# One gather fetched by SyncE row by row, subtractions in four pieces, and a tile's back transposes moved in a DLRM tower on one Trainium2 core

## What is computed

```
e = stack([tbl_f[ids[:, f]] for f in range(26)], axis=1)        # 512 x 26 x 128
combined = concatenate([e, dense[:, None, :]], axis=1)          # 512 x 27 x 128
z = einsum('bfd,bgd->bfg', combined, combined)[:, i < j]        # 351 pair products
h = concatenate([z, dense], axis=1)                             # 512 x 479
h = relu(h @ W_top1 + b_top1); h = relu(h @ W_top2 + b_top2)    # 512, then 256 wide
y = h @ W_top3                                                  # 512 x 1
```

## Time and profile before

| | us |
|---|---|
| median of 3 runs | 108.18 (108.18 to 108.19) |
| the profiled execution, device time | 108.26 |
| its span, first to last instruction | 106.4 |
| TensorE busy (granted clock full throughout) | 99.0 |
| DVE busy | 79.4 |
| ACT busy | 73.9 |
| POOL busy | 67.7 |
| 64 gathers on POOL: busy, and idle between them | 66.8 and 19.2 |

### The profile page before, as it was taken

One profiled execution on the slowest core, in us unless ns is written; L12 is line 12 of the kernel. 1 busy time (PEld: TensorE's weight loads), 2 busy tenths in 40 slices (PEclk: granted clock), 3 DMA queues, 4 the chain that ended last, 5 costly groups with the idle time before them and its releaser, 6 DMA issues.

```text
span 106.4 us, 2498 instructions
## 1 busy us (share of the span) xinstructions
PE 99.0 (93%) x998; PEld 78.6 (74%) x998; DVE 79.4 (75%) x141; ACT 73.9 (69%) x147; POOL 67.7 (64%) x72
## 2 busy tenths in 40 slices
PE   5999999999999999999989979889999985999991
PEld 1246765765686676789789967879999974899991
DVE  6899999999999999999758994951058712586120
ACT  4499999999999999999167772632257631374430
POOL 3777777777877778777777777777777773000000
PEclk9999999999999999999999999999999999999999
DMA  4861826655374654899122222111222211000000
GB/s 54 317 237 49 230 74 214 158 188 180 122 223 76 226 163 131 252 398 265 51 55 54 66 59 54 51 49 49 55 60 65 54 49 49 6 0 0 6 0 1
DMA packets 5239, 11.68 MB, mean 110 GB/s; under 512 B 1998, under 2 KB 2520, under 8 KB 5228
## 3 DMA queue, kind: packets, MB, share of 16 engines
q1 hardware_dynamic: 3160, 7.31, 21.6%
q0 software_dynamic: 2048, 4.20, 14.4%
q10 hardware_dynamic: 20, 0.02, 0.1%
HBM read 11.48 MB, written 0.00 MB: 108 GB/s over the span
## 4 chain that ended last, share of the span: by engine, by line
POOL 61%; issue 18%; PE 12%; DMA 4%; POOLq 1%; DVE 0%; ACT 0%
POOL rows L313 61%; PE gram_ps L670 3%; DMA rows<-table,ids_sb 2%; DMA ids_sb<-ids 2%; PE top_ps L737 2%; PE tr_ps L712 1%; POOLq L112 1%; PE act_ps L749 1%; PE dve_ps L749 1%; PE top_ps L762 1%; PE dve_ps L726 1%; PE dve_ps L712 1%; PE act_ps L712 1%; PE gram_ps L706 0%; PE tr_ps L683 0%
## 5 line engine op out<-in xcount | busy, mean ns | idle before, releaser
L313 POOL DMA_INDIRECT rows<-table,ids_sb x64 | 66.8, 1044 | 20.7 <-issue 19.2
L630 PE MATMUL gram_ps<-onehot,high 128*128 128x512 f32 x82 | 22.2, 405 | 0.1
L638 PE MATMUL gram_ps<-onehot,low 128*128 128x512 f32 x82 | 21.6, 406 | 0.0
L630 PEld LDWEIGHTS gram_ps<-onehot,high 128*128 128x128 f32 x82 | 14.5, 188 | 6.1 <-DVE onehot L483 2.8
L638 PEld LDWEIGHTS gram_ps<-onehot,low 128*128 128x128 f32 x82 | 14.5, 188 | 4.7 <-issue 1.8
L670 PE MATMUL gram_ps<-xt 128*58 128x52 f32 x512 | 15.1, 217 | 1.1 <-issue 1.1
L670 PEld LDWEIGHTS gram_ps<-xt 128*58 128x58 f32 x512 | 14.3, 133 | 2.0 <-issue 1.5
L483 DVE TENSOR_TENSOR onehot<-dve_ps,row_f 128x1536 fp32r<-128x1536 f32 (+1 forms) x10 | 15.2, 1524 | 0.0
L522 DVE COPY gram_sb<-gram_ps 26x208 f32<-26x208 f32 x32 | 12.0, 376 | 3.9 <-PE gram_ps L670 1.8
L483 DVE TENSOR_TENSOR onehot<-gram_ps,row_f 128x1024 fp32r<-128x1024 f32 (+1 forms) x10 | 14.8, 1478 | 0.0
L341 ACT ACTIVATE gram_sb<-gram_ps 26x208 f32<-26x208 f32 x32 | 10.7, 334 | 5.1 <-PE gram_ps L670 3.7
(11 more groups left out here) (99 smaller groups left out, 111.1 us busy)
## 6 DMA issues: line engine op xcount, KB each, us to landing
table<-table SPq DMA_DIRECT2D x9, 512.0 KB, 3.7
rows<-table,ids_sb POOLq DMA_INDIRECT x64, 2.9
w1p_sb<-w_pairs SPq DMA_DIRECT2D x1, 768.0 KB
table<-table SPq DMA_DIRECT2D x1, 640.0 KB
w_sb<-w SPq DMA_DIRECT2D x1, 512.0 KB
dense_sb<-dense SPq DMA_DIRECT2D x1, 256.0 KB, 5.8
w1d_sb<-w_dense SPq DMA_DIRECT2D x1, 256.0 KB
ids_sb<-ids SPq DMA_DIRECT2D x1, 52.0 KB, 2.0
```

What stands on the lines that cost most here:

```text
L313: pool.indirect_dma_start(rows[:, t, s - 1, :], None, tables[f], bass.IndirectOffsetOnAxis(ids_sb[:, t, f:f + 1], 0)).then_inc(gathered[t] ...
L630: pe.matmul(pick_ps[b][:], high[:, b, c, :], onehot[:, b, c, :], start=(c == 0), stop=False)
L638: last = pe.matmul(pick_ps[b][:], low[:, b, c, :], onehot[:, b, c, :], start=False, stop=(c == CHUNKS[o] - 1))
```

## The change

POOL no longer gathers slot 16 of tile 3. Its 128 rows are fetched by SP instead: the host lays the 128 ids out in a line, `ids_in_line`, which is loaded into `row_ids`; for each row SP loads one id into a register and issues a DMA of one row of 512 B at that address. Ten rows are issued ahead of the load of the third table, seven behind the load of each table from the third on, and the other 62 behind the weights. `gathered[3][4]` is waited for at 16 x 128.

The subtraction is made in 4 pieces, DVE's second one-hot instruction is split in two, and the pieces stand between the one-hot instructions. DVE's share of the shared chunk falls from 272 to 192 columns for the tables of 8 chunks. The transposes back of tile 0 go into `top_ps`, stand between the third and fourth set of `gram(1)` on TensorE, and are copied out by ACT alone. The clearing of `xt` moves: tile 2 to ACT ahead of the tables, tile 3 to DVE ahead of `gram(0)`. Three waits are finer.

```diff
-DVE_CHUNKS = {8: ((0, 1), (2, 3, 4)), 10: ((0, 1, 2), (3, 4, 5))}
-SHARED_COLS = {8: 272, 10: 368}
-DVE_PARTS = 3
+DVE_CHUNKS = {8: ((0, 1), (2,), (3, 4)), 10: ((0, 1, 2), (3,), (4, 5))}
+SHARED_COLS = {8: 192, 10: 368}
+DVE_PARTS = 4
-REST = 2
+REST = 4
+LAST_SLOT = NG
+ROWS_A_TABLE = 7
+ROWS_FIRST = 10
...
         def _(sp):
             sp.dma_start(ids_sb[:], ids.rearrange("(p t) f -> p t f", t=TILES)).then_inc(ids_in, 16)
+            def rows_by_address(at):
+                f = SLOT_FIELD[LAST_SLOT]
+                for p in at:
+                    r = sp.value_load(row_ids[0:1, p:p + 1], min_val=0, max_val=tables[f].shape[0] - 1)
+                    sp.dma_start(rows[p:p + 1, TILES - 1, LAST_SLOT - 1, :], tables[f][bass.ds(r, 1)]
+                                 ).then_inc(gathered[TILES - 1][-1], 16)
...
+                if o == TABLES:
+                    sp.wait_ge(row_ids_in, 16)
+                    rows_by_address(range(0, ROWS_FIRST))
                 if o >= TABLES:
                     sp.wait_ge(low_ready, REST * (o - TABLES + 1))
                 sp.dma_start(table[:, o % TABLES, 0:CHUNKS[o]], tables[f].rearrange("(p c) d -> p c d", c=CHUNKS[o])
                              ).then_inc(table_in[o % TABLES], 16)
                 if o == TABLES - 1:
                     sp.dma_start(dense_sb[:], dense.rearrange("(p t) d -> p t d", t=TILES)).then_inc(dense_in, 16)
+                    sp.dma_start(row_ids[:], ids_in_line).then_inc(row_ids_in, 16)
+                if o >= TABLES:
+                    rows_by_address(range(ROWS_FIRST + (o - TABLES) * ROWS_A_TABLE, ROWS_FIRST + (o - TABLES + 1) * ROWS_A_TABLE))
                 if o == WEIGHTS_AFTER:
...
+            rows_by_address(range(ROWS_FIRST + (NO - TABLES) * ROWS_A_TABLE, P))
...
                     for s in BANK_SLOTS[t][n]:
+                        if (t, s) == (TILES - 1, LAST_SLOT):
+                            continue
...
+            def back_first():
+                act.wait_ge(back_ready, 1)
+                act.activation(pairs_t[:], top_ps[:, 0:NC, :], ACT.Copy).then_inc(back_out_act, 1)
...
             def first_layer(n):
-                act.wait_ge(h1_ready, n * (N1 // P))
+                act.wait_ge(h1_ready, n * (N1 // P) - (1 if n == TILES - 1 else 2))
...
+            act.wait_ge(zeros_ready, 1)
+            act.activation(xt[:, 2, :, N_SLOTS:PAD], zeros[:, 0:1].rearrange("d (p s) -> d p s", p=1
+                                                                           ).to_broadcast([P, P, PAD - N_SLOTS]), ACT.Copy
+                           ).then_inc(pad_zero, 1)
...
-            gram(1)
-            back(1)
+            gram(1, range(SETS - 1))
+            back_first()
+            gram(1, (SETS - 1,))
...
             for o in range(NO - 1):
                 dve.wait_ge(high_ready, o + 1)
                 rest(o, 0)
...
                 whole_chunks(o + 1, 0)
                 rest(o, 1)
                 shared_chunk(o + 1)
+                rest(o, 2)
                 whole_chunks(o + 1, 1)
+                rest(o, 3)
+                whole_chunks(o + 1, 2)
...
+            dve.memset(xt[:, 3, :, N_SLOTS:PAD], 0.0).then_inc(pad_zero, 1)
             transposed(0, (3,))
...
-            dve.memset(xt[:, 2, :, N_SLOTS:PAD], 0.0).then_inc(pad_zero, 1)
             gram(1)
-            back(1)
             transposed(2, (0,))
-            dve.memset(xt[:, 3, :, N_SLOTS:PAD], 0.0).then_inc(pad_zero, 1)
...
                         pe.wait_ge(onehot_dve, DVE_PARTS * o + 3)
+                    elif c == DVE_CHUNKS[CHUNKS[o]][2][0]:
+                        pe.wait_ge(onehot_dve, DVE_PARTS * o + 4)
...
-                    pe.wait_ge(gathered[t][n], 16 * len(slots))
+                    pe.wait_ge(gathered[t][n], 16 * (P if slots[-1] == LAST_SLOT and t == TILES - 1 else len(slots)))
...
             def dense_part(t, parts=range(N1 // P)):
-                if t:
-                    pe.wait_ge(h1_out_act, 2 * t)
-                    pe.wait_ge(h1_out_dve, 2 * t)
                 ps = h1_banks(t)
                 for m in parts:
+                    if t:
+                        pe.wait_ge((h1_out_act, h1_out_dve)[m // 2], 2 * t)
...
+            def back_first():
+                pe.wait_ge(packed_act, 1)
+                pe.wait_ge(packed_dve, 1)
+                for c in range(NC):
+                    last = pe.transpose(top_ps[:, c, :], packed[:, c * P:(c + 1) * P], ident[:])
+                last.then_inc(back_ready, 1)
...
-            pe.wait_ge(pad_zero, 2)
+            pe.wait_ge(pad_zero, TILES)
...
-            gram(1)
+            gram(1, range(SETS - 1))
+            back_first()
+            gram(1, (SETS - 1,))
             transposes(2, (0, 1))
-            back(0)
             first_layer(0, range(N1 // P))
...
+        "ids_in_line": np.ascontiguousarray(a["ids"][TILES - 1::TILES, SLOT_FIELD[LAST_SLOT]].reshape(1, P)),
```

More of the change, by code:

```diff
@@ L108, with tower @@
 I32 = mybir.dt.int32
-def tower(nc, dense, ids, ids_by_field, tables, w1_pairs, w1_dense, b1, w2, b2, w3, out):
+def tower(nc, dense, ids, ids_by_field, ids_in_line, tables, w1_pairs, w1_dense, b1, w2, b2, w3, out):
     with ExitStack() as ctx:
@@ L146, in tower @@
         field_ids = sb("field_ids", [NO, B], I32)
+        row_ids = sb("row_ids", [1, P], I32)
         field_ids16 = sb("field_ids16", [P, B], F16)
@@ L183, in tower @@
         ids_in = sem("ids_in")
+        row_ids_in = sem("row_ids_in")
         dense_in = sem("dense_in")
@@ L503, in _ @@
             whole_chunks(0, 1)
+            whole_chunks(0, 2)
             for o in range(NO - 1):
@@ L651, in transposes, with gram @@
                     last.then_inc(tr_ready, 1)
-            def gram(t):
+            def gram(t, sets=range(SETS)):
                 pe.wait_ge(tr_out_dve, TR_OUT[0][t + 1])
                 pe.wait_ge(tr_out_act, TR_OUT[1][t + 1])
-                for s in range(SETS):
+                for s in sets:
                     n = t * SETS + s
@@ L686, in back @@
             def back(t):
-                pe.wait_ge(gram_out_act, max(t + 1, 2) * SETS)
-                pe.wait_ge(gram_out_dve, max(t + 1, 2) * SETS)
+                pe.wait_ge(gram_out_act, (t + 1) * SETS)
+                pe.wait_ge(gram_out_dve, (t + 1) * SETS)
                 pe.wait_ge(packed_act, t + 1)
@@ L722, in first_layer @@
                 pe.wait_ge(back_out_act, t + 1)
-                pe.wait_ge(back_out_dve, t + 1)
+                if t:
+                    pe.wait_ge(back_out_dve, t)
                 for m in parts:
@@ L813, in _ @@
             first_layer(1, range(N1 // P))
-            pe.wait_ge(pad_zero, TILES)
             gram(2)
@@ L881 @@
     out = nc.dram_tensor("y", (B, 1), F32, kind="ExternalOutput").ap()
-    tower(nc, ap["dense"], ap["ids"], ap["ids_by_field"], [ap[f"table{f}"] for f in range(N_FIELDS)],
+    tower(nc, ap["dense"], ap["ids"], ap["ids_by_field"], ap["ids_in_line"], [ap[f"table{f}"] for f in range(N_FIELDS)],
           ap["w1_pairs"], ap["w1_dense"], ap["b1"], ap["w2"], ap["b2"], ap["w3"], out)
```

## The result

| us | before | after |
|---|---|---|
| median of 4 runs | 108.19 (108.18 to 108.19) | 196.85 (196.78 to 197.52) |
| span of the profiled execution | 106.4 | 194.9 |
| TensorE busy | 99.0 | 111.7 |
| POOL's gathers, busy | 66.8 (64) | 61.7 (63) |
| last POOL gather started | 88.02 (slot 16; slot 15 at 86.77) | 82.39 (slot 15) |

The time is 1.821 times that of before (95% interval 1.817 to 1.825).

A forecast was written before the change was run, and what follows sets the result against it. POOL's gather pace, locked to DVE's subtractions, was taken as the bound, with TensorE following. From the median 108.18, -0.27 for slot 16 and +1.2 for POOL gave +0.93, so 109.1 us; 8-in-10 range 106.7 to 110.0.

The forecast's parts named there:

- SP's row cost: SP's queue: id load and issue of one row take 0.55 us, bounds 0.43 to 1.01, room up to 0.58; cost nothing.
- Rival C: SP's queue too slow from 0.58 us a row: late tables and last row, +1.5 at 0.60, 115.7 at 0.65; chance 0.10.
- POOL stays locked (+1.2): POOL's gathers in the table phase: still three a table, held by DVE's subtraction pieces; slot 15 lands 1.2 us later.
- The geometry: POOL against DVE's pieces: released gathers return after 1.25 us, the third need falling 0.06 into piece 3.
- The rule: POOL beside DVE: 0.13 us after its start a gather needs what a running subtraction holds, and continues when that ends.
- rival A: POOL slips out of step with DVE's subtractions, slot 15 lands 2 to 2.5 earlier: 106.6 to 107.6 us; chance 0.28.
- the locked case: Whole kernel with POOL's gathers still held by every subtraction pattern: 109.1 us, bounds 108.6 to 109.9; chance 0.52.
- DVE's +0.12 and ACT's +0.14 a table: Table phase: DVE's period grows 0.12 us to 4.53 from the pieces, ACT's 0.14 to 4.58 from 80 more columns.
- the table phase +1.3: TensorE's table phase ends 9 x 0.14 = 1.3 us later, late by ACT.
- Slot 16, -0.27: Tile 3's end: with slot 16 off POOL and there in time, TensorE is spared its 0.27 us wait.
- Transposes back, -1.35 and absorbed: TensorE loses waits of 0.71 and 0.64 us near 67 and 71, but then waits longer for slot 15; no gain.
- The side effects on SP: SP's queue: weights 5 us later, at about 55, still before need at 59; rows land 2 to 2.6 after issue.

## Why the prediction was wrong, by its steps

**SP's row cost: the step that failed.** The text took 0.55 us for load and issue of a row, between 0.43 and 1.01, against a room of 0.58. A row takes 1.24 to 1.26. The upper bound was the longest issue plus POOL's idle step, taken as a stand-in for a register load; the load alone is 0.49, and the address, the bounds and the gaps are 0.48 more. A row without any register operand, in contrast, is 0.30, below the lower bound: the issue was sized too high and what was not in the trace at all too low. The first ten rows had a second fault: the text lets them start at 4.3, but the line of ids has landed only at 7.1, which leaves 0.39 a row and not 0.67, and even with fixed rows the third table is issued at 11.64 instead of 10.04. The Trainium skill (DMA: Bandwidth & Descriptors, Latency and other measured facts) gives a `tensor_load` a floor of some 600 ns; the rows show 0.49, below it. The text's own estimate from that figure, over 1 us a row and about 160 us, was the nearest that it had.

**The chance given to it.** Rival C was this mechanism, with its place and its deciding point of 0.58 right: above it the tables come late and slot 16 is last, and both happened. It got 0.10, though three quarters of the text's own bounds (0.58 to 1.01 of 0.43 to 1.01) lay beyond the point. Its price was short too: "some 50 us more" at 1.01. By the same sum 1.26 gives 1.5 + 66 x 1.18 = 79; the third table's delay behind the first ten rows, which were to fit, adds 19.76 - 10.04 = 9.7, and what lies behind the long wait, the low clock and the later store, some 2.4: 91, near the 88.5 measured.

**POOL stays locked (+1.2): wrong.** The geometry was right to 0.01 us: gathers of 1.16, 1.17, and then one that comes 0.06 to 0.07 into a piece. The rule was not: a subtraction that has run for 0.07 holds nothing, and all the gathers held here and before came 0.16 or more into one. So POOL slips out of step, as rival A has it, and the change without the rows takes 107.41 where A said 106.6 to 107.6; but it slips for another reason than A's, whose five costs had to come out larger. The text saw a margin of 0.06 us in the start times, and asked only if the costs might move it, not if its rule held so close to the edge. The text's bounds have a slip too: +0.7 to +1.7 is about POOL's term alone, so that with -0.27 the locked case ends at 109.6 and not at 109.9.

**DVE's +0.12 and ACT's +0.14 a table, the table phase +1.3: the sizes right, the engine not.** In the change without the rows a piece takes 0.33 from start to start (14.25 to 14.58), DVE's period is 4.53 and ACT's 4.57 to 4.58, and the first pair products are 1.2 later. But the text had TensorE late by ACT; there TensorE's weight loads wait 4.8 us, in 15 times, for DVE's pieces and 1.4 for ACT, and the chain that ended last has 23% DVE and 1% ACT.

**Slot 16, -0.27: right but empty.** With POOL out of step the wait is gone even when POOL fetches slot 16 itself. Nothing was to be won from SP.

**Transposes back, -1.35 and absorbed: half right.** Both waits go. Left alone in front of POOL's bound they don't come out at nothing but at a loss (1.025 and 1.011 in the two sets), which no term had and whose cause stays open. The later landing of the store, 2.1 us or more instead of 1.5, is a part of it.

**The side effects on SP.** Weights at 94 us instead of about 47 cost nothing of their own, since the tables were as late. The last row landed 1.22 us after its issue, where 2 to 2.6 was taken.

## What to carry to other kernels

An instruction that no row of the trace shows is priced by measuring it alone, and until then its chance of passing a deciding point goes by how much of the bounds lies beyond it, not by the nearest familiar row; a loop that repeats it 128 times on one queue turns 0.7 us of error into 88. When a queue is stretched by another engine in a regular pattern, try moving the two apart by reordering before cutting the work up: swapping two lines put POOL out of step and gained 0.6% by the ratio, where the four pieces gained nothing. Time saved in front of an engine that still waits is worth nothing, and here it even cost a little. A low clock seen in one profile doesn't explain that by itself: look at executions of full clock, and at how much of the difference lies behind the last transfer's issue.

## What the runs showed of the hardware that was not expected

- A register load from SBUF on SP takes 0.49 us, a one-row DMA with its address from that register 1.24 to 1.26 from start to start with bounds, 0.98 without, and 0.30 at a fixed address.
- No gather that came to its operands (0.13 us after its start) within the first 0.09 us of a subtraction was held, and one that came 0.16 or more after its start was held to its end. In between, seven at 0.12 to 0.14 were not held, and the subtractions beside them took 0.04 to 0.06 longer instead; one at 0.12 was held (with fixed rows).
- Waits of TensorE of 2.18 and 2.46 us were followed by 4 us at a granted clock of 0.60 and 3 us at 0.50; one of 1.37 us was not, and neither was a pause of 2.38 us within tile 0's pair products in the trace of after, behind which the clock stayed at 1.00 from 103 to 107 us. The length of the wait alone doesn't tell:

```profile
102.80 0.40 PEld L706 LDWEIGHTS gram_ps<-xt 128*58 128x58 f32 x11 [2.38 <-issue]
```

- The store of the output (2 KB) landed 1.4 to 1.5 us after its issue in the kernel before, with the pieces alone and with the order alone, and after 2.1 to 2.4 in the nine other traces. Why stays open.
- TensorE's pause within tile 1's pair products, for which the profile names no releaser, was 0.96 us before and 0.17 with the three transposes in between:

```profile
63.98 0.93 PEld L670 LDWEIGHTS gram_ps<-xt 128*58 128x58 f32 x31 [0.96 <-issue]
```

```profile
64.40 0.93 PEld L697 LDWEIGHTS gram_ps<-xt 128*58 128x58 f32 x32 [0.17 <-issue]
```

The first is the kernel before, the second the change without rows. Why it shrinks stays open; the same edit also moves a clearing of 0.59 us away from in front of DVE's copies of these products.
